# Node rows kept, gathered and summed as two float32r parts in a two-layer graph network

## The reference

```
h = max(layernorm(x), 0);  z = h
for l in 0, 1:
    logits  = z @ envW[l] + envb[l]                      # (6250, 4)
    weights = softmax(logits)
    agg     = mean over the edges (src -> dst) of z[src] # segment sum / count
    outputs = concat(agg, z) @ W[l][k] + z, k = 0..3     # 512 x 256 each
    z       = max(sum_k weights[:, k] * outputs[k], 0)
out = x + z
```

## Time and profile before

| | |
|---|---|
| median of the runs shown | 2166.72 us (2164.43 and 2169.0) |
| the profiled execution's own time | 2174.4 us |
| its span | 2172.6 us |
| POOL busy | 1581.8 us, 73% |
| PE busy | 1784.9 us, 82% |
| DVE busy, ACT busy | 787.5 us, 257.8 us |
| moved by DMA | 256.71 MB, 118 GB/s over the span |
| mean granted TensorE clock | 0.927 |

### The profile page before, as it was taken

One profiled execution on the slowest core, in us unless ns is written; L12 is line 12 of the kernel. 1 busy time (PEld: TensorE's weight loads), 2 busy tenths in 40 slices (PEclk: granted clock), 3 DMA queues, 4 the chain that ended last, 5 costly groups with the idle time before them and its releaser, 6 DMA issues. The chain is left out here.

```text
span 2172.6 us, 32895 instructions
## 1 busy us (share of the span) xinstructions
PE 1784.9 (82%) x6096; PEld 1138.1 (52%) x6097; DVE 787.5 (36%) x2349; ACT 257.8 (12%) x728; POOL 1581.8 (73%) x1681
## 2 busy tenths in 40 slices
PE   0598888888878888888878888888888888788887
PEld 0465555555545555555535555555555555555554
DVE  4543333333333333333323333333333333333433
ACT  4411111110101101111100001010000101010100
POOL 4477777777777777777747777777777777777774
PEclk9999899998999999989969999999989999999998
DMA  7533333333333333433434344444434444444442
GB/s 241 178 113 112 110 113 112 110 113 109 113 110 111 111 112 109 113 110 112 114 111 120 114 120 117 117 119 115 120 114 120 115 119 115 120 116 117 120 115 79
DMA packets 135052, 256.71 MB, mean 118 GB/s; under 512 B 45160, under 2 KB 81795, under 8 KB 135043
## 3 DMA queue, kind: packets, MB, share of 16 engines
q0 software_dynamic: 79872, 218.21, 35.4%
q1 hardware_dynamic: 34075, 19.18, 3.2%
q10 hardware_dynamic: 21096, 19.23, 2.6%
HBM read 236.38 MB, written 19.25 MB: 118 GB/s over the span
## 5 line engine op out<-in xcount | busy, mean ns | idle before, releaser
L534 POOL DMA_INDIRECT ring<-z_dram,gather_idx x1632 | 1548.7, 949 | 517.1 <-issue 483.5
L735 PE MATMUL agg_ps<-ring,onehot 128*128 x3712 | 961.2, 408 | 306.2 <-PEq L733 265.5
L735 PEld LDWEIGHTS agg_ps<-ring,onehot 128*128 128x128 f32 x3712 | 705.3, 199 | 520.2 <-issue 433.0
L580 DVE TENSOR_TENSOR onehot<-nodes,dst_t 128x256 f32<-128x256 f32 x930 | 362.9, 420 | 393.1 <-PE agg_ps L735 244.5
L771 PE MATMUL mix_ps<-w_sb,zT 128*128 128x512 f32 x784 | 435.9, 684 | 0.0
L771 PE MATMUL mix_ps<-w_sb,meanT 128*128 128x512 f32 x784 | 352.4, 592 | 0.0
L646 DVE SCALAR_TENSOR_TENSOR mix<-mix_ps,wts,mix 128x256 f32<-128x256 f32 x392 | 189.6, 484 | 247.4 <-PE mix_ps L771 240.3
L616 DVE TENSOR_SCALAR cnt<-agg_ps 128x1 f32<-128x1 f32 x98 | 15.5, 158 | 664.1 <-PE agg_ps L735 664.1
L771 PEld LDWEIGHTS mix_ps<-w_sb,meanT 128*128 128x128 f32 x784 | 149.0, 190 | 187.5 <-issue 187.5
L771 PEld LDWEIGHTS mix_ps<-w_sb,zT 128*128 128x128 f32 x784 | 156.4, 222 | 116.0 <-issue 116.0
L689 ACT ACTIVATE ex<-logits,negmax 128x4 f32<-128x4 f32 x98 | 29.1, 297 | 1064.4 <-DVE negmax L628 1036.9
(11 more groups left out here) (72 smaller groups left out, 309.7 us busy)
## 6 DMA issues: line engine op xcount, KB each, us to landing
ring<-z_dram,gather_idx POOLq DMA_INDIRECT x1632, 2.8
z_dram<-z_res SPq DMA_DIRECT2D x7, 896.0 KB, 9.6
z_dram<-z_res ACTq DMA_DIRECT2D x49, 128.0 KB
x_in<-in_x ACTq DMA_DIRECT2D x48, 128.0 KB
out_x<-z_out ACTq DMA_DIRECT2D x48, 128.0 KB
z_res<-in_x SPq DMA_DIRECT2D x6, 896.0 KB, 13.1
w_sb<-in_L_gnn_W SPq DMA_DIRECT2D x8, 512.0 KB, 7.6
gather_idx<-src_t SPq DMA_DIRECT2D x106, 8.0 KB
```

The lines of the kernel that those rows point to most:

```text
L534: pool.indirect_dma_start(out=ring[:, s // 2, s % 2, 0:D], out_offset=None, in_=z_dram[l], in_offset=bass.IndirectOffsetOnAxis(ap=gather_i ...
L580: nc.vector.tensor_tensor(onehot[:, place, :, :], nodes[:].unsqueeze(1).to_broadcast([P, 2, P]), dst_t[:, bass.ds(u * 2, 2)].unsqueeze(2). ...
L735: mm = pe.matmul(agg_ps[:, :], onehot[:, place, h, :], ring[:, bass.ds(u % RING, 1), h, 0:D + 1], start=first and h == 0, stop=True, skip_ ...
```

## The change

Every node row is kept as two parts, a high part in float32r (a float32 rounded to fewer bits of mantissa) and a low part, the float32 value less the high one, so that the two add up to the value. A row in `z_dram` and in a slot of `ring` is now 2 KB: 256 columns high, 256 columns low, and in the ring two columns of ones. The one-hot matrices are float32r, and each tile is added to `agg_ps` by two float32r matmuls, one of 258 columns (low part and ones), one of 256 columns (high part).

In the first stage ACT computes each tile twice, once into the high part of a slot and once in place; DVE subtracts to get the low part (`low_parts`), for group `g` behind the scales of group `g + 1`. The parts of the node tiles go through ring slots 16 to 31, seven slots for even and seven for odd groups, and so ACT waits, before it begins group `g` (2 to 6), until the store of group `g - 2` has landed; SP's stores take the slots in place of `z_res` and wait for the low parts. Only 16 tiles are gathered early (`EARLY`), into the space of layer 1's weights (`raw`), and their parts go into slots 0 to 15; 16 gathers for slots 16 to 31 follow from `z_dram[0]` in place of 8. In layer 0's main loop each block has one more activation on ACT and one more instruction on DVE, into `parts`, which is stored in place of the `z_res` rows.

```diff
@@ -32,15 +32,16 @@
 I32 = mybir.dt.int32
+F32R = mybir.dt.float32r
 LN_EPS = 1e-5
 RING = 16
-ROW = 264
+ROW = 520
 NO_NODE = 1 << 20
 TURN = 4
 PLACES = 2 + (TURN - 1) + TURN
 LOAD = 7
-EARLY = 24
+EARLY = 16
@@ -73,7 +74,7 @@
     with ctx:
-        z_dram = [nc.dram_tensor(f"z{l}_dram", (NB * P, D), F32).ap() for l in range(L)]
+        z_dram = [nc.dram_tensor(f"z{l}_dram", (NB * P, 2 * D), F32).ap() for l in range(L)]
@@ -81,7 +82,8 @@
         envb_sb = sb("envb_sb", [1, L, K])
-        ring = sb("ring", [P, RING, 2, ROW])
+        ring = sb("ring", [P, RING, 2, ROW], F32R)
+        parts = sb("parts", [P, 2 * D], F32R)
         ident = sb("ident", [P, P])
@@ -95,7 +97,7 @@
         unsorted = sb("unsorted", [1, 2])
-        onehot = sb("onehot", [P, PLACES, 2, P])
+        onehot = sb("onehot", [P, PLACES, 2, P], F32R)
         z_in = sb("z_in", [P, D])
@@ -110,7 +112,7 @@
-        agg_ps = psum("agg_ps", [P, D + 1])
+        agg_ps = psum("agg_ps", [P, D + 2])
         zT_ps = psum("zT_ps", [P, DC, P])
@@ -144,6 +146,10 @@
         s_h = sem("h_computed")
+        s_high = sem("h_high_part_ready")
+        s_low = sem("h_low_part_ready")
+        s_hi1 = sem("z1_high_part_ready")
+        s_lo1 = sem("z1_low_part_ready")
@@ -205,6 +211,8 @@
             warm = ed("warm", [1, 1])
+            raw = w_sb[:, L - 1, :, :, :].rearrange("p c k o -> p (c k) o")
+            slots = ring[:].rearrange("p v h r -> p (v h) r")
@@ -235,7 +243,7 @@
                 pool.indirect_dma_start(
-                    out=ring[:, s // 2, s % 2, 0:D], out_offset=None, in_=table,
+                    out=raw[:, s, :] if s < EARLY else ring[:, s // 2, s % 2, 0:2 * D].bitcast(F32), out_offset=None, in_=table,
                     in_offset=bass.IndirectOffsetOnAxis(ap=src_t[:, s:s + 1], axis=0),
@@ -245,7 +253,13 @@
             def rows(t):
-                return z_res[:, t, :] if t < NB else ring[:, (t - NB) // 2, (t - NB) % 2, 0:D]
+                return z_res[:, t, :] if t < NB else raw[:, t - NB, :]
+
+            def split(t):
+                if t >= NB:
+                    return slots[:, t - NB, 0:2 * D]
+                return slots[:, EARLY + (t // LOAD) % 2 * LOAD + t % LOAD, 0:2 * D]
+
@@ -279,9 +293,10 @@
                         a, b = xrange(g)
-                        sp.wait_ge(s_h, b)
+                        sp.wait_ge(s_low, b)
+                        first = EARLY + g % 2 * LOAD
                         sp.dma_start(z_dram[0][a * P:b * P, :].rearrange("(t p) d -> p t d", p=P),
-                                     z_res[:, a:b, :]).then_inc(s_hst[g], 16)
+                                     slots[:, first:first + b - a, 0:2 * D].bitcast(F32)).then_inc(s_hst[g], 16)
                     load_weights(sp, 0)
@@ -304,7 +319,7 @@
                     nc.gpsimd.memset(ones_col[:], 1.0).then_inc(s_const, 1)
-                    nc.gpsimd.memset(ring[:, :, :, D:D + 1], 1.0).then_inc(s_const, 1)
+                    nc.gpsimd.memset(ring[:, :, :, 2 * D:2 * D + 2].bitcast(F32), 1.0).then_inc(s_const, 1)
                     nc.gpsimd.memset(eps[:], LN_EPS).then_inc(s_const, 1)
@@ -407,6 +422,14 @@
                     due = [max(XG - 3 + i, 1) for i in range(len(pieces))]
+                    def low_parts(g):
+                        a, b = groups[g]
+                        for t in range(a, b):
+                            dve.wait_ge(s_high, t + 1)
+                            dve.wait_ge(s_h, t + 1)
+                            nc.vector.tensor_tensor(split(t)[:, D:2 * D], rows(t), split(t)[:, 0:D],
+                                                    ALU.subtract).then_inc(s_low, 1)
+
                     for g in range(len(groups)):
@@ -415,6 +438,9 @@
                             compare_pairs()
+                        else:
+                            low_parts(g - 1)
+                    low_parts(len(groups) - 1)
                     dve.wait_ge(s_bias, 1)
@@ -435,6 +461,10 @@
                                 roots(g + 1)
+                            if t == a and 2 <= g < XG:
+                                act.wait_ge(s_hst[g - 2], 16)
+                            nc.scalar.activation(split(t)[:, 0:D], rows(t), ACT.Relu,
+                                                 bias=nbias[:, t:t + 1], scale=rstd[:, t:t + 1]).then_inc(s_high, 1)
                             nc.scalar.activation(rows(t), rows(t), ACT.Relu,
@@ -517,7 +547,7 @@
                         if l:
-                            pool.wait_ge(s_stored[l - 1], 16 * NB)
+                            pool.wait_ge(s_stored[l - 1], 16 * NB + 16)
                         else:
@@ -532,7 +562,7 @@
                                 pool.indirect_dma_start(
-                                    out=ring[:, s // 2, s % 2, 0:D], out_offset=None, in_=z_dram[l],
+                                    out=ring[:, s // 2, s % 2, 0:2 * D].bitcast(F32), out_offset=None, in_=z_dram[l],
                                     in_offset=bass.IndirectOffsetOnAxis(ap=gather_idx[:, s:s + 1], axis=0),
@@ -651,6 +681,11 @@
                                                                    op0=ALU.max, op1=ALU.add).then_inc(s_res, 1)
+                                else:
+                                    dve.wait_ge(s_hi1, now)
+                                    nc.vector.scalar_tensor_tensor(
+                                        out=parts[:, D:2 * D], in0=mix[:], scalar=0.0, in1=parts[:, 0:D],
+                                        op0=ALU.max, op1=ALU.subtract).then_inc(s_lo1, 1)
@@ -670,6 +705,8 @@
                             act.wait_ge(s_res, base)
+                        if not last:
+                            act.sem_inc(s_stored[l], 16)
                         take_z(0)
@@ -701,11 +738,13 @@
                                     act.sem_inc(s_past, 1)
+                                    act.wait_ge(s_stored[l], blk * 16 + 16)
+                                    nc.scalar.activation(parts[:, 0:D], mix[:], ACT.Relu).then_inc(s_hi1, 1)
                                     nc.scalar.activation(z_res[:, bass.ds(blk, 1), :], mix[:],
                                                          ACT.Relu).then_inc(s_res, 1)
-                                    act.wait_ge(s_res, now)
+                                    act.wait_ge(s_lo1, now)
                                     act.dma_start(z_dram[l + 1][bass.ds(blk * P, P), :],
-                                                  z_res[:, bass.ds(blk, 1), :]).then_inc(s_stored[l], 16)
+                                                  parts[:].bitcast(F32)).then_inc(s_stored[l], 16)
                                 else:
@@ -732,9 +771,11 @@
                             for h in range(2):
-                                mm = pe.matmul(agg_ps[:, :], onehot[:, place, h, :],
-                                               ring[:, bass.ds(u % RING, 1), h, 0:D + 1],
-                                               start=first and h == 0, stop=True, skip_group_check=True)
+                                slot = ring[:, bass.ds(u % RING, 1), h, :]
+                                pe.matmul(agg_ps[:, :], onehot[:, place, h, :], slot[:, :, D:2 * D + 2],
+                                          start=first and h == 0, stop=True, skip_group_check=True)
+                                mm = pe.matmul(agg_ps[:, 0:D], onehot[:, place, h, :], slot[:, :, 0:D],
+                                               start=False, stop=True, skip_group_check=True)
                                 if h == 1:
```

## The result

The changed kernel takes **2218.34 us** (2217.81 and 2218.87) against 2166.72 before: ratio 1.0238, 95% interval 1.0191 to 1.0286, slower. The forecast was 2218. The profiled execution took 2217.81 us, its span is 2216.0.

The account below looks back on a forecast made before the run. POOL's gathers, one every 1.253 us, were taken to bound the kernel. First stage +42, eight more gathers +10.0 and turns -0.6 made +51.4 us on 2166.7, so 2218 us; range 2190 to 2265.

Parts of the forecast that it names:

- What bounds: Main loops: POOL's gathers, one every 1.253 us, set the time; the halved matmul on PE hides behind them.
- Pitch 0: POOL's gather in the main loops: 2 KB rows add 0 to its 949 ns; bounds 0 and +949 ns.
- the rival by packets: POOL's time for a gather goes by packets: +633 ns, 3261 us; part of the dearer-gather rival, chance 0.12.
- Queues: DMA in the loops: transfers hide behind POOL, q0 at about 70% of the engines, 85% occupancy at most, landing 0.5 us later.
- the rival by queues: DMA queues become the bound: at 1.35 us for 2 KB rows the pitch rises by 0.1, 2380 us; chance 0.03.
- Eight gathers, +10.0: Layer 0: EARLY 16 in place of 24 leaves 816 gathers behind the first stage in place of 808, +10.0 us.
- The first stage, +42: Before the main loops: doubled activations and waits for stores delay the first gather to 118.9 us, +42; bounds +14 and +54.
- Layer 0's blocks, 0: Layer 0's main loop: the extra ACT and DVE instructions, up to 1.0 us a block, fit PE's slack; cost 0.
- The turns, -0.6: Uncovered ends of the layers: +0.4 us between them, about -1.0 at the end, -0.6 in all.
- What would show it: Trace signs: gathers 949 ns and 1.253 us apart, q0 about 70%, first gather at 119 us, PE's busy share down some 200 us.
- The sum: Whole kernel: 42 + 10.0 - 0.6 = +51.4 us on the median 2166.7, giving 2218 us, 2.4% slower.
- PE as the bound, and the clock: Rival: PE too slow in the loops, 2600 us if float32r is not one pass, 2522 at 1.2 GHz; chance 0.03.

Follow-up runs that it names:

- e2: Changed kernel with the main loops' gathers cut back to 1 KB rows, so other values are summed: 2214.99 us, 2.5 less than the changed kernel.
- e1: Kernel before with the matmul change alone, rows still 1 KB float32, one float32r matmul of 258 columns for a tile: 2169.04 us against 2166.82, ratio 1.0009.
- e5: Changed kernel with its two matmuls for a tile taken as float32: 2910.64 us, on a chip that gave the kernel before at 3177.32.
- e11: Changed kernel with its two matmuls for a tile taken as float32, run again: 2859.59 us, on a chip that gave the kernel before at 3196.70.
- e3: Kernel before with EARLY 16 in place of 24, nothing else: 2170.74 us, +3.9, ratio 1.0014.
- e4: Changed kernel, unaltered, run again beside the kernel before on one chip: 2217.47 us against 2166.82 over 19 runs.
- e12: Kernel before with EARLY 32 and the last group of x loaded ahead of the shifted edge list: 2162.80 us against 2168.63, ratio 0.9978.
- e8: Kernel before with EARLY 32 and the last group of x loaded ahead of the shifted edge list: 3193.6 us, on a chip with the kernel before at 3177.
- e9: Changed kernel with four sets of seven ring slots in place of two for the first stage's parts: 3228.5 us; kernel before there 3166.
- e7: Kernel before with EARLY 32 in place of 24: 3195.9 us, on a chip that gave the kernel before at 3177.

## Why the prediction was right, step by step

- **What bounds**: right. POOL's step is 1.25 us with rows of 1 and of 2 KB (e2) and with all, half or a quarter of the matmul work on the pairs (e1), and no total moves by more than 2.5 us with either. How much more work PE could take is not shown (e5, e11).
- **Pitch 0**: right, 948 against 949 ns; so was the packet count, and thus the rival by packets (+633 ns) is out. The Trainium skill (DMA: Bandwidth & Descriptors, section SWDGE vs HWDGE vs iDMA) has one read and one write descriptor made for each DMA operation and names no size in bytes for it. If a row is such an operation, their number stays at 2 KB; the trace agrees as far as POOL's time shows it, 948 against 949 ns, while the bytes that q0 moved went from 218.21 to 434.22 MB.
- **Queues**: 67.6% forecast as about 70, total 76% in the loops under the bound of 85. Landing was 0.9 us later, not 0.5. In the rival by queues the price was too low: it left out the up to 0.15 us of q1 and q10 that stood in the bound, so 1.35 us of q0 would be 1.50 and not 1.35 against 1.253. It did not come to that.
- **Eight gathers, +10.0**: 9.7 in the trace, and e3's total agrees with it.
- **The first stage, +42**: the mechanism was right, down to which groups wait, and the size was off by 7.5 us. Store 0 was issued at 44.3 and landed at 53.7 in place of 57; a store alone landed after 6.6 us in place of 8.1, which I had built from a queued rate and a latency that partly overlap; an ACT group took 7.1 us in place of 7.4. Group 4 so began at 69.2 (74.5), group 6 at 84.8 (92.0), and ACT was done at 107.9 (116.0).
- **Layer 0's blocks, 0**: right to about 1 us. The step in layer 0 is no longer than in the profile before (1.2528 against 1.2532), and e4's layer is 1.2 us longer than e3's.
- **The turns, -0.6**: +1.1, and +3.4 between e3 and e4. The halved pairs gave what was forecast, 0.9 us between the layers and 1.3 at the end. But the last pair began 0.5 and 0.9 us later behind the last gather, and between the layers the longer way to the store (+0.7) and the larger store (+0.3) came on top, about as forecast. At the end the first four dense products took 3.74 us in place of 2.87: the granted clock over them was 0.50, where before it had risen in their course (0.66). Between the layers it is 0.50 in both kernels. The forecast had left the clock of the dense part out of this term.
- **What would show it**: two items were off. The first gather of the main loops came at 111 us, not 119, as above. PE's busy time fell by 91 us, not by some 200; the clock took back part of the gain, 33 us on the experts' products alone in 150 to 1050 us.
- **The sum**: the hit to the microsecond is luck. The terms were 8 us too large against the two traces, and the profiled execution before was itself 7.7 us over its median, while the one after lay 0.5 below its own; the forecast had subtracted the 7.7 from both sides. Against the medians (+51.6, and +50.7 in e4) the terms fit because errors cancel. The pair of e3 and e4 shows which: the stage was forecast about 7 us too long, the two turns 4.0 us and layer 0's blocks 1.2 us too short.
- **PE as the bound, and the clock**: the forecast expected PE to fall to 1.2 GHz more often and still to stay inside its slack; it did, at 0.81 in the change and at 0.74 in e1. The Trainium skill (TensorE: Matmul & The Clock Gate, section Part 1) has idle stretches throttle the array. The trace agrees, with 0.50 at the pairs that come one by one, and the time did not follow, since PE was not the bound.

## What to carry to other kernels

Before making an engine's work cheaper, find the instruction whose start-to-start time never varies: here a gather every 1.25 us on POOL. With rows of 1 or 2 KB, and with a quarter to all of the matmul work, its step did not move; what counted was how many gathers lie outside the cover of another stage. A change made for the loop is paid for in the preparation: there look for buffers that are reused behind a store, and for the order in which one queue issues loads and stores. The ends of a stage, where nothing covers a landing or a matrix engine at its lower clock, want terms of their own. And a profile is one execution: a step that differs by 3 ns is 5 us after 1640 of them, so compare small differences over many runs, not between two traces.

## What the runs showed of the hardware

- The indirect gather takes 945 to 950 ns on POOL (means of stretches) and 0.30 us to the next, for 128 rows of 1 KB or of 2 KB, with 48 or 80 packets.
- Its step differs between executions, 1.2499 to 1.2546 us, by layer and run.
- A float32r matmul of 256 or 258 columns starts 0.12 us after the one before at 2.4 GHz and 0.21 at 1.2 GHz; four for a pair are 0.48 us against 0.91 in float32.
- The chips of e1 to e4 and of e12 gave the kernel before at 2166.8 and 2168.6 us. Those of e5 to e8 and of e9 to e11 gave the same program at 3166 to 3197 us. In e7's trace from there DVE waits 11 us on average, 43 at most, for a signal whose sender the trace does not find; what is slow was not found.
